# VectorE's statistics and rsqrt of the second FFN half's rows, split over four units

## The reference

```python
h = _layernorm(x, axis=-1) * (1 + ca) + sa
x = x + ga * _L0_attn_ref(h, ...)           # causal attention
h = _layernorm(x, axis=-1) * (1 + cb) + sb  # the layer norm of this case
x = x + gb * _L0_ffn_ref(h, ...)            # gated FFN, 704 wide, 8 LoRA adapters, top 2

def _layernorm(x, axis=-1, eps=1e-05):
    m = jnp.mean(x, axis=axis, keepdims=True)
    v = jnp.var(x, axis=axis, keepdims=True)
    return (x - m) / jnp.sqrt(v + eps)
```

## Time and profile before

| | |
|---|---|
| time, median of 3 runs | 689.21 us (688.83 to 689.48) |
| the profiled execution | 688.73 us, its span 686.9 us |
| granted TensorE clock, mean | 0.994 of full speed |
| TensorE matmul busy | 652.9 us, 95% |
| VectorE busy | 474.2 us, 69% |
| ScalarE busy | 356.7 us, 52% |
| GpSimd busy | 377.4 us, 55% |

### The profile page before, as it was taken

The page is one execution under the profiler, slowest core; times in us unless marked ns, Lnnn a source line. Parts: engine busy times, 40 slices in busy tenths (PEclk is TensorE's granted clock), DMA queues, the critical chain, the costliest instruction groups (busy, mean ns, idle before and its releaser), DMA issues.

```text
span 686.9 us, 10710 instructions
## 1 busy us (share of the span) xinstructions
PE 652.9 (95%) x3772; PEld 558.8 (81%) x3772; DVE 474.2 (69%) x1146; ACT 356.7 (52%) x642; POOL 377.4 (55%) x473
## 2 busy tenths in 40 slices
PE   4869999999999999999999999999999999999996
PEld 3559987888879987888878897798888998788885
DVE  5997678478886677658976767747987657637323
ACT  4635455546455546465455446564454546654543
POOL 3785345538577236647576516654765635543644
PEclk9989999999999999999999999999999999999999
DMA  8300020000000020000000001000000000000000
GB/s 311 122 1 1 1 62 0 1 2 31 0 2 31 1 62 0 1 1 32 0 1 32 1 1 62 0 1 18 15 1 1 32 1 1 0 1 1 31 0 32
DMA packets 14054, 15.45 MB, mean 22 GB/s; under 512 B 1328, under 2 KB 12720, under 8 KB 14000
## 3 DMA queue, kind: packets, MB, share of 16 engines
q1 hardware_dynamic: 14000, 14.76, 6.4%
HBM read 10.57 MB, written 4.19 MB: 21 GB/s over the span
## 4 chain that ended last, share of the span: by engine, by line
PE 82%; DVE 12%; issue 2%; POOL 2%; DMA 1%; ACT 1%; DVEq 0%; SPq 0%
PE ps L1263 76%; PE ps L1272 6%; DVE xr L856 2%; DVE hid L1103 1%; DVE rstd L829 1%; DVE zb L844 1%; DMA xs<-in_L_attn_x 1%; DVE xT_lo L890 1%; POOL ring_lo L469 1%; DVE mv L836 1%; DVE tr_full L856 1%; ACT act_s L709 1%; DVE zb L927 0%; DVE stat L841 0%; DVE nr_a L827 0%
## 5 line engine op out<-in xcount | busy, mean ns | idle before, releaser
L469 POOL TENSOR_TENSOR ring_lo<-hid,ring_hi 128x512 fp32r<-128x512 f32 x144 | 189.3, 1319 | 115.9 <-ACT ring_hi L717 115.2
L1103 DVE TENSOR_TENSOR hid<-act_s,ps 128x512 f32<-128x512 f32 x120 | 81.9, 684 | 82.0 <-ACT act_s L709 81.4
L709 ACT ACTIVATE act_s<-ps 128x512 f32<-128x512 f32 x120 | 71.7, 597 | 123.0 <-PE ps L1263 122.4
L717 ACT ACTIVATE ring_hi<-hid 128x512 fp32r<-128x512 f32 (+1 forms) x144 | 90.3, 627 | 16.2 <-DVE hid L1101 8.7
L461 POOL TENSOR_TENSOR xT_lo<-tr_full,xT_hi 128x512 fp32r<-128x512 f32 x28 | 35.9, 1297 | 33.5 <-ACT xT_hi L588 33.5
L1263 PE MATMUL ps<-wdT_hi,ring_hi 128*128 128x256 f32 x192 | 53.6, 285 | 0.0
L1263 PE MATMUL ps<-wdT_lo,ring_hi 128*128 128x256 f32 x192 | 53.2, 282 | 0.0
L1263 PE MATMUL ps<-wdT_hi,ring_lo 128*128 128x256 f32 x160 | 45.2, 282 | 0.0
L1263 PE MATMUL ps<-tm_hi,bgT_hi 128*128 128x512 f32 x96 | 39.5, 411 | 5.7 <-DVE hid L1103 5.7
L1263 PE MATMUL ps<-vv_hi,pT_hi 128*128 128x256 f32 x144 | 43.3, 301 | 0.0
L476 POOL TENSOR_TENSOR xr<-xr,y_gb 128x256 f32<-128x256 f32 x31 | 22.1, 739 | 34.2 <-DVE y_gb L1138 34.2
(11 more groups left out here) (229 smaller groups left out, 2026.4 us busy)
## 6 DMA issues: line engine op xcount, KB each, us to landing
xs<-in_L_attn_x SPq DMA_DIRECT2D x4, 1024.0 KB, 5.6
out<-xr SPq DMA_DIRECT2D x7, 512.0 KB, 3.0
s_mod<-in_L_wmod SPq DMA_DIRECT2D x1, 1024.0 KB, 8.8
s_qkvT<-in_L_attn_qkv SPq DMA_DIRECT2D x1, 768.0 KB, 10.3
s_wg<-in_L_ffn_Wg SPq DMA_DIRECT2D x1, 704.0 KB, 7.4
s_wu<-in_L_ffn_Wu SPq DMA_DIRECT2D x1, 704.0 KB, 8.6
s_wd<-in_L_ffn_Wd SPq DMA_DIRECT2D x1, 640.0 KB, 7.3
s_mod<-in_L_wmod SPq DMA_DIRECT2D x1, 512.0 KB, 6.9
```

The lines of the kernel that those rows point to most:

```text
L469: pool.tensor_sub(ring[1][:, place(n), :], hid[:, n % HID, :], ring[0][:, place(n), :].bitcast(fp32)).then_inc(h_lo.sem, 1)
L709: nc.scalar.activation(act_s[:, n % 2, :], ps[:, 2 * (n % 2), :], ACT.Silu).then_inc(silu_ready.sem, 1)
L717: nc.scalar.activation(ring[0][p0:P, place(n), :], hid[p0:P, n % HID, :], ACT.Copy).then_inc(h_hi.sem, 1)
L1103: V.tensor_mul(hid[:, n % HID, :], act_s[:, n % 2, :], ps[:, 2 * (n % 2) + 1, :]).then_inc(h_ready.sem, 1)
```

## The change

The bodies of the instructions stay as they are. The Newton rounds get a function of their own, and the block that stood behind the product of unit 5 is cut into four: `bn_stats` of the last tile behind unit 2, `bn_aggr` and `neg_mean` behind unit 3, the guess and one Newton round behind unit 4, the other two rounds and `shift` behind unit 5.

```diff
+            def newton(lo, n, rounds):
                 v, a, y = nr_v[:, lo:lo + n], nr_a[:, lo:lo + n], rstd[:, lo:lo + n]
-                link(guess(lo, n))
-                for _ in range(NEWTON):
+                for _ in range(rounds):
                     link(V.tensor_mul(a, y, y))
                     link(V.scalar_tensor_tensor(a, a, -0.5, v, ALU.mult, ALU.mult))
                     link(V.scalar_tensor_tensor(y, a, 1.5, y, ALU.add, ALU.mult))
+
+            def rsqrt(lo, n):
+
+                link(guess(lo, n))
+                newton(lo, n, NEWTON)
...
                 for r in range(2, UPC):
                     hidden(r)
-                    if r == 5:
+                    if r == 2:
                         x1_stats(TC + 3)
+                    if r == 3:
                         moments(range(TC, NT))
                         mark(V.tensor_scalar(neg_mean[:, TC:NT], mv[:, TC:NT, 0], -1.0, None, ALU.mult))
-                        rsqrt(TC, TC)
+                    if r == 4:
+                        link(guess(TC, TC))
+                        newton(TC, TC, 1)
+                    if r == 5:
+                        newton(TC, TC, NEWTON - 1)
                         dve.sem_inc(norm_ready.sem, 1)
                         V.tensor_mul(shift[:, TC:NT], neg_mean[:, TC:NT], rstd[:, TC:NT]).then_inc(rstd_ready.sem, 1)
```

More of the change, by code:

```diff
@@ L820, in guess @@
                 return V.tensor_scalar(y.bitcast(i32), nr_i[:, lo:lo + n], -1.0, float(0x5f3759df), ALU.mult, ALU.add)
-            def rsqrt(lo, n):
+            def newton(lo, n, rounds):
                 v, a, y = nr_v[:, lo:lo + n], nr_a[:, lo:lo + n], rstd[:, lo:lo + n]
-                link(guess(lo, n))
-                for _ in range(NEWTON):
+                for _ in range(rounds):
                     link(V.tensor_mul(a, y, y))
```

## The result

The changed kernel takes 694.28 us (median of six runs, 693.67 to 697.35) against 689.15 us of the kernel before beside it.

What follows compares the result with a forecast made beforehand. TensorE bounds the kernel (82% of the chain), waiting four times for VectorE's hid. Gate holds delaying the logits, 3 x 1.27 - 0.4 = +3.4 us, give 692.1 on the profiled execution, 692.6 by medians; range 688.4 to 693.8.

Steps and rivals of the forecast that it cites:

- `neg_mean` behind unit 3: VectorE: held by GpSimd's subtraction, ends at 103.52; next product starts at 103.44; TensorE's unit 6 late by 0.27 us.
- Unit 4's piece: VectorE: nr_v ends at 105.01, first Newton instruction held until 106.73; product of unit 5 at 107.15; TensorE's unit 7 1.18 late.
- Unit 5's piece: VectorE: fifth Newton instruction gets in, sixth stands until 109.90; product of unit 6 ends at 110.84; TensorE's unit 8 0.22 earlier.
- ScalarE's chain and the turn at L875: Activation of unit 8 0.25 later; GpSimd's unit 9 subtraction precedes the gate instruction (L871 before) by 0.13, ending it 1.27 later.
- TensorE at the logits: Router logits 1.27 us later in each of the first three batches; fourth batch gains 0.4; sum +3.4 us.
- the 0.35: Extra length of the fourth batch's TensorE wait at unit 8; if it goes too, that batch gains up to 0.57.
- I count on nothing later to take this back: Behind an FFN half TensorE waits for VectorE's normalisation, a chain that moves with TensorE: no lateness recovered.
- L875 getting in first: Rival: gate instruction precedes GpSimd's unit 9 subtraction, only ScalarE's 0.25 reaches the logits: +0.35, 689.6 us; chance 0.28.
- The rival of the pieces that fit: Pieces fit VectorE's idle time before units 3 to 5: 684.4, all of it 682.5, a third 687 us; chance 0.17.
- The 6.75 given as the most: TensorE's four waits for hid at unit 8, 3 x 1.60 + 1.95 us: the most the change could give.
- Whether `nr_v` would pass: VectorE, unit 4: passing GpSimd despite its strided input would end the product of unit 5 0.20 earlier; taken as held.

Runs made afterwards that it cites:

- e3_filled_wait: Changed kernel with five 128x512 matmuls that feed nothing filling TensorE's wait ahead of the router logits in the first three batches: 692.23 us, ratio 1.0046.
- e9_last_gate_late: Changed kernel with only the last gate instruction, L875, moved from behind unit 9 to behind unit 13: 687.38 us, ratio 0.9977.
- e2: Changed kernel with the next batch's gate instructions moved from behind units 8 and 9 to behind units 12 and 13: 687.43 us, ratio 0.9978.
- e6: Kernel before with only the gate instructions moved from behind units 8 and 9 to behind units 12 and 13: 688.46 us, ratio 0.9993.
- e1: Only the statistics moved early (bn_stats behind unit 2, bn_aggr behind unit 3), the rest of the burst left behind unit 5: 688.86 us, ratio 0.9999.
- e10: Changed kernel with GpSimd's subtractions of units 2 to 5 cut to 8 columns and the gates behind units 12 and 13: 681.34 us, ratio 0.9892.
- e8: Kernel before with the burst cut once, two Newton rounds and shift behind unit 6, and gates behind units 12 and 13: 681.81 us, ratio 0.9897.
- e5_short_sub: Changed kernel with GpSimd's subtractions of units 2 to 5 cut from 512 to 8 columns, their down projections reading ring_hi: 692.75 us, ratio 1.0045.
- e4_late_xT: Kernel before with four idle bn_stats added ahead of tr_full behind unit 10 in the first three batches: 698.65 us, ratio 1.0137.
- e7_split_5_6: Kernel before with the burst cut once, last two Newton rounds and shift behind unit 6, gates where they were: 690.43 us, ratio 1.0045.

## Why the prediction was half right

The changed kernel's first batch starts 0.68 us later than that of the kernel before (product of unit 3 at 102.32 instead of 101.64): its profiled execution is slower in the set-up. Times below are less 0.68.

- **`neg_mean` behind unit 3**: ends at 103.52, as predicted; the next product starts at 103.43 (103.44). TensorE's unit 6 is late by 0.3 (0.27 was taken, although the times that the prediction gives for the product's end, 103.81 and 104.13, are 0.32 apart; nothing in the sum hangs on it). Its weight load has this row:

```profile
104.84 0.19 PEld L1272 LDWEIGHTS ps<-xT_hi,wgT_hi 128*128 128x128 f32 x1 [0.41 <-DVE hid L1107]
```

- **Unit 4's piece**: `nr_v` ends at 105.01 (105.01), the first Newton instruction is held, and the product of unit 5 starts at 107.16 (107.15). TensorE's unit 7 starts at 107.90 (107.90).
- **Unit 5's piece**: the fifth Newton instruction gets in, by 0.05 us, the sixth ends at 109.90 (109.90), the product of unit 6 starts at 110.15 and ends at 110.84 (110.84).
- **ScalarE's chain and the turn at L875**: the activation of unit 8 is at 113.00 (113.05), GpSimd's subtraction at 117.90 (117.95), L875 at 118.02 (118.08), and it ends at 119.74 (119.80). The order of the two turned round as said, by 0.12 us (0.13).
- **TensorE at the logits**: late by 1.21 in a batch (1.27). The fourth batch gained 0.21, not 0.4: its wait was longer before, but no part of the 0.35 came back. Together 3 x 1.21 - 0.21 = +3.4, as predicted (3.4); e3_filled_wait, which has these waits and no low clock, measured 3.2.
- **The step that failed** is the one from the waits to the time: "I count on nothing later to take this back". I asked only what would give time back, not what the new wait of 0.93 us would do to the stage behind it. The sum priced every TensorE instruction behind the wait as before. In the profiled executions two of three batches ran them at half clock for a while, 1.5 to 3.1 us each; over the runs it comes to 5.1 - 3.4 = 1.7 us, or 2.0 against e3_filled_wait, which has the same waits and keeps the clock. That term is what was put at nothing without a reason. So the range ended at the sum of waits plus 0.3 per batch, and the time lay 0.5 us above.
- **The rivals.** L875 getting in first lost by 0.12 us. No run shows what it would have been. e9_last_gate_late is not that case: with L875 gone from there, the product of unit 10 starts 0.5 us earlier than in the kernel before (118.65 in e9's timeline, 117.90 on the time scale of the kernel before, against 118.44), while L875 in front would have put it 0.25 later. So the price of 689.6 stays open. What e2 and e9 gain over the kernel before, 1.6 us, is more than four times the 0.22 gained at unit 8. From the first logits of the first batch to the last of the fourth, e2 takes 515.85 us (86.02 to 601.87) where the kernel before takes 517.37: 0.42 less in each of three batches and 0.24 in the fourth. The gates' move alone gives 0.46 in the same stretch (e6), and 4 x 0.22 with it makes 1.3 of the 1.52. The rival of the pieces that fit was rightly low: with GpSimd in their way they don't (e1, e2), and with it out of their way the gain of 6.1 us appears (e10 against e2). The 6.75 given as the most is confirmed by the place where they do fit: 6.65 (e8 against e6).

The Trainium skill (SBUF — State Buffer, Who interferes with whom) was cited for the shared port pair, where the second of the two engines fully blocks. e5_short_sub agrees on the blocking: shorten GpSimd's instruction, and `neg_mean` falls from 0.86 to 0.17 us in the same place. That a port is the reason, no run here can show. Whether `nr_v` would pass was left to the rows; with 0.98 us it doesn't.

Open: why some batches keep the upper clock behind the same wait of 0.93 us. Neither the length of this wait nor the width of the matmuls behind it was varied.

## What to carry to other kernels

In this kernel VectorE's idle time between two products is where GpSimd works on the product before, so small SBUF instructions cut into such gaps stand there for up to a whole GpSimd instruction; put in them what was seen to pass (statistics, products with an input in PSUM), and order the rest by GpSimd's turns and not by the sum of lengths. When a change moves two engines by tenths of a microsecond, look further down for every pair of VectorE and GpSimd instructions whose order may turn, and remove that pair before a gain is counted: here the place of one instruction of 0.69 us decided between 694.3 and 687.4 us, and that of the whole group of gate instructions between 690.4 and 681.8. A new TensorE wait of about 1 us may cost more than itself, as the one ahead of the narrow router matmuls did here: put the clock behind it into the range.

## What the runs showed of the hardware

- TensorE's granted clock fell from full to half (1.2 GHz) behind a wait of 0.93 us followed by the router's 128x16 and 128x8 matmuls: in two of three batches, and not the same ones in two executions; behind waits of 1.0 us in e4_late_xT in three of three; in one of three in the profiles of e5_short_sub and e7_split_5_6, with waits of 0.93 and 0.94 us; in none when the wait was filled with matmuls. In the kernel before, the waits of 1.33 and 1.68 us ahead of 128x512 matmuls, at unit 8, left it at 1.00 in all four batches. Each stretch cost 1.5 to 3.1 us, more than the wait.
- A VectorE instruction of four columns with a strided input, `neg_mean` or `nr_v`, is held by GpSimd as the others are: 0.86 and 0.98 us, against 0.17 and 0.19 with the subtraction shortened.
- How close a turn can be: the fifth Newton instruction behind unit 5 started at 109.22, 0.05 us ahead of a subtraction, and took 0.16; the first Newton instruction behind unit 4, 0.10 us behind one, took 1.21 us; L875, 0.12 us behind one, took 1.72 us for 0.69 us of work.
